# Scaling attention probabilities on GpSimd ahead of their transposes, and an output projection in three products of parts, in a fused two-layer kernel

## The reference, cut to what matters

```
p[h]   = exp(scores[h] - max)              # 384 x 384, causal
o[h]   = (p[h] @ v[h // 4]) / (1 + sum(p[h]))
x      = x + concat(o) @ Wo                # 1024 x 256
```

## Time and profile before

| what | value |
|---|---|
| median of 3 runs | 1914.97 us (1912.51 to 1917.04) |
| span of the profiled execution | 1913.2 us |
| its time beside the span | not given by the profile; the runs are within 4 us of it |
| layer 0's attention units | to about 760 us |
| layer 1's attention units | about 760 to 1280 us |
| epilogue, routing, experts | 1280 to 1913 us |

### The profile page before, as it was taken

How to read it: one execution, slowest core, us unless ns; L and a number is a source line. 1 busy time by engine, 2 the same in 40 slices (tenths; PEclk the granted TensorE clock), 3 DMA queues, 4 the chain that set the end, 5 groups by cost and what they waited for, 6 DMA issues and landing times.

```text
span 1913.2 us, 33649 instructions
## 1 busy us (share of the span) xinstructions
PE 1771.8 (93%) x11231; PEld 1431.5 (75%) x11231; DVE 1232.3 (64%) x4073; ACT 968.2 (51%) x2669; POOL 544.9 (28%) x763
## 2 busy tenths in 40 slices
PE   5787999999999999899999999992999999999997
PEld 3455677776867677677887878862898998999896
DVE  6667677786867675756767777667854545454452
ACT  1355657575766766565576666640233334333421
POOL 2241434324242410111111111011425333533431
PEclk8687999999999999999999999996989999999998
DMA  6111010101101010103011110002222221222210
GB/s 209 39 37 62 3 62 1 62 1 61 36 11 59 1 34 1 34 1 94 1 35 34 34 34 2 26 26 85 86 75 92 99 71 40 82 79 67 64 40 21
DMA packets 74243, 91.03 MB, mean 48 GB/s; under 512 B 16523, under 2 KB 64310, under 8 KB 74072
## 3 DMA queue, kind: packets, MB, share of 16 engines
q1 hardware_dynamic: 61464, 67.90, 11.0%
q0 software_dynamic: 9472, 16.77, 3.2%
q10 hardware_dynamic: 3136, 4.21, 0.6%
HBM read 71.02 MB, written 25.00 MB: 50 GB/s over the span
## 4 chain that ended last, share of the span: by engine, by line
PE 72%; issue 10%; DVE 8%; POOL 2%; ACT 2%; DMA 2%; DVEq 1%; POOLq 1%; SPq 1%; ACTq 0%
PE bank L1605 16%; PE bank L1034 16%; PE bank L1620 9%; PE bank L982 6%; PE bank L1017 6%; PE bank L966 5%; PE bank L938 3%; PE bank L1194 2%; PE bank L1056 2%; PE bank L993 1%; PE bank L918 1%; PE bank L939 1%; DVE probs L2290 1%; DVE at_least L2913 1%; POOLq L3139 1%
## 5 line engine op out<-in xcount | busy, mean ns | idle before, releaser
L1729 ACT ACTIVATE probs<-probs,nmax 128x128 f32<-128x128 f32 (+2 forms) x768 | 381.1, 502 | 64.2 <-DVE nmax L2290 64.1
L982 PE MATMUL bank<-cst,probs 128*128 128x128 f32 x1536 | 234.9, 279 | 20.9 <-ACT probsT L1737 9.1
L982 PEld LDWEIGHTS bank<-cst,probs 128*128 128x128 f32 x1536 | 180.0, 142 | 53.9 <-issue 15.4
L1605 PE MATMUL bank<-xeT,gate_w 128*128 128x480 f32 x768 | 187.6, 379 | 0.5 <-issue 0.5
L1605 PE MATMUL bank<-xeT,up_w 128*128 128x480 f32 x768 | 187.1, 379 | 0.0
L2433 DVE COPY probsT<-bank 128x384 f32<-128x384 f32 x256 | 141.1, 551 | 65.1 <-PE bank L982 64.3
L1620 PE MATMUL bank<-down_w,hT 128*120 128x256 f32 x1536 | 181.3, 280 | 0.0
L1620 PEld LDWEIGHTS bank<-down_w,hT 128*120 128x120 f32 x1536 | 179.9, 181 | 0.1
L3076 DVE TENSOR_TENSOR prod<-bank,sil 128x480 f32<-128x480 f32 x128 | 84.1, 657 | 147.7 <-PE bank L1605 126.0
L3182 POOL COPY rinv<-rowsum 128x384 f32<-128x384 f32 x80 | 40.7, 509 | 480.7 <-DVE o1T L2312 289.9
L1737 ACT COPY probsT<-bank 128x384 f32<-128x384 f32 x256 | 121.8, 476 | 108.8 <-PE bank L982 100.0
(11 more groups left out here) (350 smaller groups left out, 3420.3 us busy)
## 6 DMA issues: line engine op xcount, KB each, us to landing
gate_raw<-in_L_ffn_gate_w SPq DMA_DIRECT2D x8, 1024.0 KB
up_raw<-in_L_ffn_up_w SPq DMA_DIRECT2D x8, 1024.0 KB
down_raw<-in_L_ffn_down_w SPq DMA_DIRECT2D x8, 1024.0 KB, 5.7
img<-in_x SPq DMA_DIRECT2D x8, 768.0 KB
residual_rows<-x SPq DMA_DIRECT2D x8, 384.0 KB
residual_rows<-h_in SPq DMA_DIRECT2D x8, 384.0 KB
xr<-residual_rows SPq DMA_DIRECT2D x8, 384.0 KB, 4.4
hr<-residual_rows SPq DMA_DIRECT2D x8, 384.0 KB, 3.8
```

What stands on the lines that cost most here:

```text
L982: last = tr(ps[bank][:, P * q:P * (q + 1)], probs[:, n % 4, SEG[t] + P * j:SEG[t] + P * (j + 1)], ident)
L1605: last = mm(ps[bank][:, 0:HALF], w[:, wp, c, P * m:P * (m + 1)], xeT[:, xp, c, HALF * hf:HALF * (hf + 1)], start=(c == 0 and k == 0), stop ...
L1729: last = f(p, p, ACT.Exp, bias=nmax[:, n % 4, t:t + 1], scale=-1.0, accum_out=rowsum[:, where, t:t + 1])
```

## The change

In layer 1 the probabilities are scaled before they are transposed. GpSimd's `scale(n)` multiplies a head's three pieces of `probs` with the reciprocals in `rowsum`, in place, and the transposes wait for it (`probs_scaled`) in place of `exp_done`. `spread`, `divisors` and `take_divisors` are gone from layer 1; in layer 0 they stay. Bank 5 is copied by ScalarE to `o1_hi` as fp32r (`take_out`), and VectorE writes the rest to `o1_lo` (`lower_out`, in `weigh`'s place) and frees the bank. `wo1` is split too, once, at the end of `U_EIGHT`, and the projection runs as three products of parts a chunk. All statement lists are in a new order, layer 0's too, and `dense_units` with them; buffers are placed over others that are free by then.

```diff
+        unused_start = first_only + 4 * (2 * S + NT * KV1 * HD1)
...
-        (o1T,), o1_end = region(first_end, ("o1T", [P, 8, S], F32))
+        (o1_hi,), o1_end = region(first_end, ("o1_hi", [P, 8, S], F32R))
         assert o1_end <= offsets["top"]
+        wo0_start = offsets["top"]
...
+        (wo1_raw,), _ = region(mlp_start, ("wo1_raw", [P, 8, D], F32))
+        (wo1_lo,), _ = region(mlp_start, ("wo1_lo", [P, 8, D], F32R))
+        (wo1_hi,), _ = region(f1T_start, ("wo1_hi", [P, 8, D], F32R))
...
+        spare_start = offsets["top"]
+
+
+        o1_lo = [region(at_, (f"o1_lo{c}", [P, S], F32R))[0][0] for c, at_ in enumerate(
+            (unused_start, spare_start, rows_start, rows_start + 4 * S, rows_start + 8 * S, wo0_start,
+             w2_start, w2_start + 4 * S))]
+        assert 3 * S <= 5 * D and 2 * S <= 4 * D
...
+                def load_out_weights():
+                    if k is U_EIGHT:
+                        banks.wait_taken(sp, SEC_EIGHT, f"up0_{FM - 1}")
+                        wo1_src = a["L1_attn_Wo"].rearrange("(g s r d) n -> g s d r n", g=2, s=2, r=4, d=HD1)
+                        for g in range(2):
+                            for s in range(2):
+                                sp.dma_start(wo1_raw[64 * s:64 * s + 64, 4 * g:4 * g + 4, :], wo1_src[g, s]) \
+                                    .then_inc(wo1_loaded, 16)
+
...
                     load_second()
+                    load_out_weights()
                     store_rows()
                     load_sums()
                     store_normed()
...
-            wo1_src = a["L1_attn_Wo"].rearrange("(g s r d) n -> g s d r n", g=2, s=2, r=4, d=HD1)
-            for g in range(2):
-                for s in range(2):
-                    sp.dma_start(wo1[64 * s:64 * s + 64, 4 * g:4 * g + 4, :], wo1_src[g, s]).then_inc(wo1_loaded, 16)
             sp.dma_start(route_c[:], const[:, ROUTE_COLS:NC_COLS]).then_inc(route_loaded, 16)
...
             def probs_transposed(n, u, half):
 
                 bank = 3 + half
-                if half == 0:
+                if half == 0 and u[1] < B:
                     pe.wait_ge(exp_done, at(u, HEADS, n + 1))
+                elif half == 0:
+                    pe.wait_ge(probs_scaled, at(moved(u, -B), HEADS, n + 1))
                 pe.wait_ge(freed[bank], at(u, HEADS, take0[bank] + n))
...
+            def out_pieces(c, t):
+                cols_t = slice(P * t, P * (t + 1))
+                return [(x[:, cols_t], w[:, c, :]) for x, w in (
+                    (o1_hi[:, c], wo1_hi), (o1_hi[:, c], wo1_lo), (o1_lo[c], wo1_hi))]
...
-                    if k.tail is not None:
-                        denominators_transposed(sec, i, "rinvT_tail", k.tail, moved(u, -1), (1, 7)[k.tail])
+                    if k.tail == 0:
+                        denominators_transposed(sec, i, "rinvT_tail", 0, moved(u, -1), 1)
...
                 def second_rows(t):
                     if k.s3:
                         if t == 0:
-                            pe.wait_ge(wo1_loaded, 64)
+                            pe.wait_ge(wo1_split, 1)
                             pe.wait_ge(freed[5], at(img_a, PAIRS, take0[5] + 2 * B + PAIRS))
-                        token_major(sec, i, "proj1", t, o1T, wo1, 8)
+                        product(sec, i, f"proj1_{t}", [piece for c in range(PAIRS) for piece in out_pieces(c, t)], D)
...
                 else:
+                    scores(1)
+                    divisors_last()
+                    mix_last()
+                    values(0)
                     turn(0, 0)
-                    scores(1)
                     turn(0, 1)
-                    mix_last()
-                    divisors_last()
+                    attn_rows(0)
+                    second_rows(0)
                     turn(1, 0)
...
                     ffn_up(3)
                     ffn_up(4)
+                    turn(15, 0)
                     ffn_up(5)
-                    turn(15, 0)
                     ffn_up(6)
+                    turn(15, 1)
                     ffn_up(7)
-                    mix(6)
-                    turn(15, 1)
-                    router()
-                    second_queries(7)
                     ffn_down(0)
                     ffn_down(1)
                     ffn_down(2)
+                    second_queries(7)
+                    router()
...
-                        last = mm(ps[bank][:, 0:D], o1T[:, c, P * t:P * (t + 1)], wo1[:, c, :],
-                                  start=(c == 0), stop=(c == PAIRS - 1))
+                        for q, (x, w) in enumerate(out_pieces(c, t)):
+                            last = mm(ps[bank][:, 0:D], x, w, start=(c == 0 and q == 0),
+                                      stop=(c == PAIRS - 1 and q == 2))
...
             rows_out(range(PAIRS - 2), (2,))
-            denominators_transposed(EPI, 0, "rinvT_tail", 1, last_u, PAIRS - 1)
             pe.wait_ge(freed[5], take0[5] + 2 * B + PAIRS * B - 1)
             rows_out((PAIRS - 2,))
             pe.wait_ge(freed[5], take0[5] + 2 * B + PAIRS * B)
...
+            def upper_out(u, c):
+                act.wait_ge(probs_used, used_index(1, u, c + 1))
+                nc.scalar.copy(o1_hi[:, c, :], ps[5][:, 0:S]).then_inc(out_upper, 1)
+
...
+                def take_out(c):
+                    upper_out(u, c)
+
+                def take_out_last():
+                    if k.tail == 1:
+                        upper_out(moved(u, -1), PAIRS - 1)
+
+                def out_weights_upper():
+                    if k is U_EIGHT:
+                        act.wait_ge(wo1_loaded, 64)
+                        nc.scalar.copy(wo1_hi[:].rearrange("p c n -> p (c n)"), wo1_raw[:].rearrange("p c n -> p (c n)")) \
+                            .then_inc(wo1_upper, 1)
...
                 else:
                     exps(0)
                     exps(1)
+                    take_divisors_last()
+                    take_out_last()
+                    exps(2)
                     take_turned(0)
-                    take_divisors_last()
-                    take_divisors(0)
...
+            def lower_out(u, c):
+
+                dve.wait_ge(out_upper, at(moved(u, -B), PAIRS, c + 1))
+                tt(o1_lo[c][:], ps[5][:, 0:S], o1_hi[:, c, :].bitcast(F32), ALU.subtract).then_inc(freed[5], 1)
 
             def queries_keys_of(sec, i, t):
...
+                    if k.layer == 0:
+                        weigh_of(sec, i, f"rinvT{c}", 0, u, c)
+                    else:
+                        lower_out(u, c)
 
                 def weigh_last():
-                    if k.tail is not None:
-                        weigh_of(sec, i, "rinvT_tail", k.tail, moved(u, -1), (1, 7)[k.tail])
+                    if k.tail == 0:
+                        weigh_of(sec, i, "rinvT_tail", 0, moved(u, -1), 1)
+                    elif k.tail == 1:
+                        lower_out(moved(u, -1), PAIRS - 1)
+
+                def out_weights_lower():
+                    if k is U_EIGHT:
+                        dve.wait_ge(wo1_upper, 1)
+                        flat_w = lambda z: z[:].rearrange("p c n -> p (c n)")
+                        tt(flat_w(wo1_lo), flat_w(wo1_raw), flat_w(wo1_hi).bitcast(F32), ALU.subtract).then_inc(wo1_split, 1)
 
                 def take_first():
...
-                    take_turned(3)
                     second_norm(2)
+                    gray_ahead()
                     attn_rows(2)
+                    take_queries_keys(0)
...
                 else:
                     invert_last()
+                    invert(0)
                     mask_max(2)
+                    weigh_last()
                     mask_max(3)
-                    invert(0)
-                    weigh_last()
                     take_turned(0)
                     take_values(0)
+                    attn_rows(0)
+                    invert(1)
+                    take_turned(1)
+                    mask_max(4)
+                    mask_max(5)
                     second_moments(0)
...
+                    take_turned(2)
+                    take_values(1)
+                    invert(2)
+                    mask_max(6)
...
-                    moe_rows(2)
+                    invert(3)
                     weigh(0)
-                    invert(2)
...
-                    take_turned(8)
-                    weigh(2)
+                    moe_norm(1)
+                    weigh(3)
+                    moe_norm(2)
+                    take_turned(9)
+                    invert(5)
...
                     take_turned(13)
+                    invert(7)
+                    mask_ahead(0)
...
-                    take_queries(7)
                     ffn_rows(0)
+                    out_weights_lower()
                     ffn_rows(1)
-                    take_logits()
                     take_turned(15)
                     ffn_rows(2)
-                    weigh(6)
+                    take_logits()
+                    take_queries(7)
...
```

(71 more changed lines are left out.)

498 lines of the change are left out of this document (236 added, 262 removed).

## The result

The changed kernel takes 1891.66 us in the median of 4 runs (1890.57 to 1896.1). The kernel before, measured beside it, takes 1913.74 us. The ratio is 0.9883, 95% interval 0.9862 to 0.9903: 22.1 us faster, where 30.5 was forecast. The forecast time was 1884.5 us, its range 1868 to 1903.

The account below looks back on a forecast made before the run. TensorE, busy 58.82 of a middle unit's 59.08 us, was taken as the bound. Middle units 24.0, image 0's unit 2.0, Wo wait 1.6, last unit 1.0, epilogue 1.9, layer 0 0: 1914.97 - 30.5 = 1884.5 us, range 1868 to 1903.

Parts of the forecast that it names:

- Divisors and new wait: Layer 1 middle unit: dropping transposed divisors saves TensorE 3.2 us; waiting for the scaling costs 0.7 (0 to 1.5).
- the prediction's tight spot: Start of a layer 1 unit: 5.6 us of TensorE work must cover 5.4 us up to the scaling; 0.4 wait given.
- Projection: Layer 1 output projection: 24 fp32r products take 2.95 us a tile against 3.46, saving 1.5 us a unit.
- GpSimd's scaling: Layer 1: three instructions a head of about 0.30, 0.40 and 0.51 us, 1.2 us a head.
- A middle unit: Layer 1: each gains 4.7 less 0.7, so 4.0 us; six gain 24.0.
- Image 0's unit, last unit, epilogue: Layer 1's ends: gains of 2.0 us, 1.6 for the Wo load wait, 1.0 and 1.9.
- Layer 0: Same work in another order on all queues: taken as 0 us, though new 2 us waits would lose 14.
- rival B: Layer 0's new order loses 2 us in each of six units, giving 1896.5 us; chance 0.14.
- layer 0's unit unchanged within 1 us: Sign that the forecast is right; a layer 0 unit differing by more would mean it is wrong.
- Rival A: Layer 1 scaling at the two-input rate, 2.2 us a head, loses 12 us, giving 1896.5; chance 0.14.
- Rivals C and D: C: GpSimd becomes layer 1's bound, 1938 us, chance 0.08; D: products at 0.216 us each, about 1930, chance 0.04.

Follow-up runs that it names:

- e6: Changed kernel with the scaling kept but the output projection back in 8 f32 products a tile, without the split; 1899.73 us, ratio 0.9919.
- e5: Changed kernel without the scaling of every head's second and third piece on GpSimd, all products kept; 1880.58 us, ratio 0.9833.
- e11: Changed kernel with every head's pieces of 128 and 256 columns multiplied a second time, by 1.0, on GpSimd; 1918.6 us, ratio 1.0021.
- e4: Changed kernel with all three pieces of every head multiplied a second time, by 1.0, on GpSimd; 1971.6 us, ratio 1.0282.
- e1: Changed kernel with gray_ahead() in layer 0 moved back behind take_values(0), from behind second_norm(2); 1877.52 us, ratio 0.9808.
- e2: Changed kernel with all layer 0 lists in the order of the kernel before, layer 1 new; 1883.45 us, ratio 0.9839.
- e3: Changed kernel without the product of o1_hi and wo1_lo, 16 products a tile in place of 24; 1881.64 us in one run.
- e9: Changed kernel, layer 0 mixed: new lists with early gray_ahead() in the first and last two units, old lists in U_MID0; 1868.62 us, ratio 0.9767.
- e7: Kernel with old layer 0 lists and new layer 1, with gray_ahead() moved behind second_norm(2); 1937.29 us, ratio 1.0139.
- e10: Changed kernel without the o1_hi and wo1_lo product and without scaling every head's second and third piece; 1881.47 us, ratio 0.9815.

## Why the prediction came out as it did

The forecast was 8 us too good, inside its range. Its mechanism in layer 1 held, its zero for layer 0 did not, and 3.9 us of chance in the routing and the experts hid a part of that. By its own steps:

- **Divisors and new wait.** Forecast 3.2 less 0.7 = 2.5 us a middle unit; 59.1 - 56.7 = 2.4 with the scaling alone (e6). The wait was put at 0.7: what e5 gives back with 1.07 of the 1.47 us a head gone is 0.8. The size is right, the way to it in part luck: the five units show no wait for GpSimd at all, not at `turn(0, 0)` either, and the price shows only when the work is taken out. With more scaling (e11) `turn(0, 0)`, the prediction's tight spot, is one of four, with 0.7 of 3.2 us; the turns of heads 12, 14 and 15 were not seen.
- **Projection.** 2.95 us a tile, to the digit; 1.5 us a unit forecast, 1.2 measured (1.4 in the last two). The fp32r rows of `ffn_down` carried over. The split of the weights took 1.9 us on ScalarE and 2.3 on VectorE, once, with 2.6 and 2.9 as the forecast's upper bounds.
- **GpSimd's scaling.** 0.30, 0.40 and 0.51 us forecast, 0.39, 0.49 and 0.60 measured, so 1.47 us a head and not 1.2. The slope a column, (597 - 386) / 256 = 0.82 ns, is that of the copy in the earlier trace rows; the fixed part is 0.28 us where 0.19 was taken. The second multiplication in e4 has a literal in place of the column `rowsum` and takes 0.30, 0.42 and 0.51, where the first takes 0.38, 0.48 and 0.59 in the same trace: the factor in a column is 0.06 to 0.08 of the missing 0.09. The Trainium skill (GPSIMD Engine Reference, Elementwise — side-by-side cycle accounting) gives 1.03 cycles an element for bodies of one or two operations, from which 0.86 ns at 1.2 GHz is an estimate; the trace's slope of 0.82 agrees. The rest of the 1.47 is the three fixed parts.
- **A middle unit** therefore gained 3.5 us on average (3.8 in the fourth and fifth), with 4.0 forecast: six gave 20.9 of 24.0.
- **Image 0's unit, last unit, epilogue.** 6.5 forecast, 7.5 measured, with the split not to be read from the stores. PE's 1.6 us wait for `Wo` is gone. In its place stands PE's wait for the scaling, 2.9 us (longest 1.9), up to the first `xn_rows`; the last unit and the epilogue have 0.5 more.
- **Layer 0** is the step that failed: "a new wait of 2 us in each ... loses 14. I take 0." The prediction even named VectorE's `gray_ahead` behind the norms, and did not follow it through SyncE's halo loads to the convolution, its user in the same unit. The wait is 2.5 us a unit, rival B's mechanism, where B had 2. A full unit became 3.3 us longer, 1.9 of it by the late gray image and 1.4 by the rest of the order (e1, e2). Up to the seventh store the loss is 9.2 us, since the new order is better in the last two units (80.6 and 77.2 against 84.5 and 79.7); by the medians of e2 and the changed kernel it is 8.2. The sign "layer 0's unit unchanged within 1 us" called it: 88.8 against 85.4. With layer 0 as before (e2) the gain is 30.3 us, against 30.5 forecast. That agreement is better than the single terms: by its trace the six middle units are 2.8 us short of their 24.0, and image 0's unit, the last and the epilogue 2.8 over their 6.5.
- **Routing and experts** gave 3.9 us that no step had. Their work is the same; TensorE's clock is not. In the first expert the kernel before has 20 us at a mean of 0.74, the changed one at 0.91 (first row before, second after):

```profile
1390.00:1410.00 20.00, 20.00 (x89) 17.86 (x88) 8.48 (x13) 4.61 (x9) 10.15 (x8) 0.74 0.18 43
```

```profile
1370.00:1390.00 20.00, 20.00 (x105) 17.69 (x105) 10.32 (x15) 5.88 (x12) 9.50 (x8) 0.91 0.33 95
```

  2 x 0.26 x 20 = 10.4 and 3.6 us at the lower clock: half of the difference is 3.4. From `gate_raw` to the end e2 takes 613.0, e6 613.1, e1 611.5, e3 610.0, e9 609.8 us. So this part scatters by 3 us between kernels that don't differ in it, and nothing shows the 3.9 to be a gain of the change: it is taken for chance.
- **Rival A** took 2.2 us a head for a loss of 12 us and 1896.5. e11 has that size, and gives 1918.6: 26.9 more than the changed kernel. The rival was named, its price was less than half. The slack that the prediction worked out (10.6 us for the odd head, of 13.6) isn't there at four places of the list. What a head may take seems to be set there, place by place, by the order of the lists, and not by the mean pace of pairs. That is argued from the places of e11's waits, and no kernel tested it.
- **Rivals C and D** did not come. The scalings have a longest of 0.99 us and a mean of 0.49, so GpSimd is hardly held up. The hold that C named is there, but falls on VectorE: normalisations beside a scaling take 0.58 and 0.68 us instead of 0.41, 0.5 us a unit. The products run at 0.123.

## What to carry to other kernels

When a hand-written order changes, follow each moved producer through its DMA to its first user, and read the distance in us from the trace: here 7.5 us later on VectorE became 2.5 us of wait on TensorE in every full unit, and one statement put back gave 14 us. Judge an order by kind of unit: the one that wins in a full unit loses in one that lacks a part, and the mix beat both by 9 and 15 us (e1 and e2). And a boundary that is easy to find in a trace, such as a store, need not be where a unit's list begins: place a wait by the statement it stands at. Slack on a helper engine is not its idle time: GpSimd was idle for over half of the unit, and 0.7 us more a head took the whole gain away.

## What was not expected of the hardware

A wait on TensorE can cost more than itself. In e7, 4.5 us of wait for a load brought up to 13.4 us at half clock and 10 us a unit; in the changed kernel's full units, 2.5 us of wait left the clock whole. Nor is 2.5 us safe: e4 has the same layer 0 as the changed kernel, statement for statement, and in two of its units the granted clock fell to 0.94 and 0.92,

```profile
444.00:533.00 89.00, 83.99 (x505) 61.35 (x504) 63.53 (x219) 53.62 (x156) 30.40 (x51) 0.94 0.10 32
533.00:622.00 89.00, 84.33 (x495) 61.11 (x493) 61.20 (x209) 51.34 (x150) 30.40 (x51) 0.92 0.08 25
```

which made them 93.5 and 94.8 us long instead of 88.8. The waits there are no longer than the changed kernel's, 2.5 and 2.2 us, and in the first of the two the fall stands right behind:

```profile
461.43 1.56 PE L949 MATMUL bank<-gray,band 128*128 128x256 f32 x6 [2.55 <-issue]
...
464.06 2.93 PE L949 MATMUL bank<-gray,band 128*128 128x256 f32 x6
```

e3, e6 and e10, with the same layer 0, have a shorter fall right behind the wait of 2.5 to 2.7 us in the first full unit (its mean is 0.98); e5 and e11 have none in their full units. What decides between the two stays open. On GpSimd, a `tensor_scalar` with its factor in a column takes 0.06 to 0.08 us longer than one with a literal, at all three widths (e4: means of 379, 481 and 591 ns against 300, 418 and 514). And a scaling on GpSimd can make a normalisation on VectorE that runs beside it last 0.58 to 0.68 us instead of 0.41, although the two share no data.
